# Three projection stages: transposes and matmuls by pairs of tiles, the bias on GpSimd, two banks for the heads' sums

## What is computed

```python
def _L0_attn_ref(x, qkv_w, qkv_b, proj_w, proj_b, rpb_table):
    ...
    attn = jax.nn.softmax(attn + bias[None], axis=-1)
    out = jnp.einsum('bhnm,bmhd->bnhd', attn, v).reshape(Bw, Nw, Cd)
    return out @ proj_w + proj_b
...
h = h + _L0_attn_ref(_layernorm(h, axis=-1), ...)      # stage prj
h = h + _L1_attn_ref(_layernorm(h, axis=-1), ...)      # linear attention, stage lpr
x = x + y @ wo.T                                       # causal attention in _L1_ffn_ref, stage cpj
```

## Time and profile before

| what | value |
|---|---|
| median of 3 runs | 2918.41 us (2917.83 to 2937.95) |
| profiled execution, own time | 2931.52 us |
| its span | 2929.7 us |
| TensorE busy (PE) | 2564.9 us, 88% |
| weight loads (PEld) | 1160.8 us, 40% |
| DVE, ScalarE (ACT), GpSimd (POOL) busy | 1987.7, 1552.4, 354.0 us |
| granted TensorE clock, mean | 0.887 of full speed |

### The profile page before, as it was taken

The page is one execution under the profiler, slowest core; times in us unless marked ns, Lnnn a source line. Parts: engine busy times, 40 slices in busy tenths (PEclk is TensorE's granted clock), DMA queues, the critical chain, the costliest instruction groups (busy, mean ns, idle before and its releaser), DMA issues. The chain is left out here.

```text
span 2929.7 us, 52672 instructions
## 1 busy us (share of the span) xinstructions
PE 2564.9 (88%) x18552; PEld 1160.8 (40%) x18552; DVE 1987.7 (68%) x5083; ACT 1552.4 (53%) x2645; POOL 354.0 (12%) x456
## 2 busy tenths in 40 slices
PE   5987659999999999997699997986679998789999
PEld 3323542333333333335333333564544444623333
DVE  5686668888888888871477775737667774256665
ACT  2332654777777777772244443615646666134443
POOL 1020100000000000003112211011101011221110
PEclk9998767999999999996699997755589999589999
DMA  2101991112212212213300001233422231511100
GB/s 72 22 15 27 279 281 51 48 45 55 56 38 56 55 38 55 70 17 85 67 17 17 22 16 24 61 85 124 160 104 72 66 91 35 123 28 29 29 15 20
DMA packets 308491, 188.23 MB, mean 64 GB/s; under 512 B 262069, under 2 KB 263414, under 8 KB 306982
## 3 DMA queue, kind: packets, MB, share of 16 engines
q1 hardware_dynamic: 297870, 165.80, 21.4%
q0 software_dynamic: 10368, 19.06, 2.1%
HBM read 103.16 MB, written 81.69 MB: 63 GB/s over the span
## 5 line engine op out<-in xcount | busy, mean ns | idle before, releaser
L1614 DVE TENSOR_REDUCE att_mpart<-ps 128x1 f32<-128x512 f32 x1024 | 637.3, 684 | 81.2 <-PE ps L1423 48.5
L1571 ACT ACTIVATE att_p<-ps 128x704 f32<-128x704 f32 x768 | 543.3, 760 | 139.5 <-PE ps L1487 134.5
L1516 PE MATMUL ps<-att_p,att_v 128*32 128x352 f32 x3072 | 308.4, 472 | 0.1
L1423 PE MATMUL ps<-att_kT,att_qT 64*128 64x512 bf16 x1024 | 274.5, 387 | 27.5 <-DMA att_qz<-qt_d 14.2
L1487 PE MATMUL ps<-att_qm,att_kT 64*128 64x352 bf16 x1536 | 251.1, 317 | 10.8 <-ACT att_p L1571 8.0
L1243 DVE TENSOR_REDUCE cau_mpart<-ps 128x1 f32<-128x512 f32 (+5 forms) x384 | 193.5, 552 | 90.8 <-PE ps L1069 70.7
L2285 ACT ACTIVATE mo_act<-ps,mo_b 128x768 f32<-128x768 f32 x176 | 156.3, 901 | 129.5 <-PE ps L2167 129.5
L2478 DVE TENSOR_TENSOR mo_g<-mo_act,ps 128x768 f32<-128x768 f32 x176 | 167.4, 951 | 79.5 <-PE ps L2202 43.5
L1210 ACT ACTIVATE cau_p<-ps 128x704 f32<-128x704 f32 (+6 forms) x272 | 171.6, 660 | 82.5 <-PE ps L1128 49.7
L2865 ACT ACTIVATE mo_act<-ps 128x1024 f32<-128x1024 f32 (+1 forms) x108 | 102.9, 953 | 196.3 <-PE ps L2779 196.0
L1487 PEld LDWEIGHTS ps<-att_qm,att_kT 64*128 64x128 bf16 x1536 | 82.4, 93 | 279.8 <-issue 263.6
(11 more groups left out here) (432 smaller groups left out, 4367.2 us busy)
## 6 DMA issues: line engine op xcount, KB each, us to landing
v_d<-pre_v SPq DMA_DIRECT2D x32, 288.0 KB, 4.3
qs_d<-pre_qs SPq DMA_DIRECT2D x8, 1152.0 KB, 5.6
att_qs<-qs_d SPq DMA_DIRECT2D x32, 288.0 KB, 4.5
att_v<-v_d SPq DMA_DIRECT2D x32, 288.0 KB, 4.4
qt_d<-pre_qT SPq DMA_DIRECT2D x8, 1056.0 KB, 4.4
kt_d<-pre_kT SPq DMA_DIRECT2D x8, 1056.0 KB, 7.6
att_kT<-kt_d SPq DMA_DIRECT2D x32, 264.0 KB, 2.7
att_qT<-qt_d SPq DMA_DIRECT2D x32, 264.0 KB, 3.1
```

The source lines that it names most:

```text
L1423: mm = pe.matmul(ps[:, bank, :], qT[half(s), u, j * P:(j + 1) * P], kT[half(s), u, c * BANK:(c + 1) * BANK], start=True, stop=not near)
L1516: mm = pe.matmul(ps[32 * cg:32 * cg + 32, 7, 0:TH], v[:, u, i, s, :], p[:, r, s, :], start=i < 2, stop=i == FULL - 1)
L1571: e = act.activation(p[:, n % PRING, :, :], ps[:, bank:bank + 2, 0:TH], ACT.Exp)
L1614: red = dve.tensor_reduce(mpart[:, j, s, c:c + 1], ps[:, bank, :], AX.X, ALU.max)
```

## The change

It changes `project` in five ways. (1) `turn` transposes two neighbouring tiles of `att` at once, 128 partitions by 128 columns: four transposes and a small one instead of eight and a small one. Of each pair, channels of the even tile land on partitions 0 to 63 and those of the odd one on 64 to 127, in one bank. (2) `back` weighs the two halves as two row tiles of the array: `w` is loaded to both halves of the partitions, the matmuls alternate between them, and their outputs go to banks 4 and 5. The number of matmuls stays. ScalarE copies 128 partitions by 512 and the small piece. (3) The ones and the bias row are gone; GpSimd adds the bias, spread over all partitions, into the residual rows before DVE needs them, and DVE waits for that. (4) The heads' sums get a second pair of banks, 6 and 7, by turns. (5) front(b + 1) stands ahead of turn(b).

```diff
...
@@ -1659,19 +1658,21 @@
         den = nm.sb("den", [P, 2, NT, heads])
         rden = nm.sb("rden", [P, 2, NT, heads])
         att = nm.sb("att", [P, 2, NT, C])
-        xT = nm.sb("xT", [P, 2, N])
+        xT = nm.sb("xT", [P, 2, BANK + TT])
         w = nm.sb("w", [P, C])
+        bias = nm.sb("bias", [P, C]) if bias_d is not None else None
...
         block = const["block"]
-        XT, Y = 2, 5
+        FRONT, XT, Y = (0, 6), 2, 4
+        PAIRS = FULL // 2
...
@@ -1697,9 +1698,10 @@
 
         def fetch(sp):
             load(sp, 0, 0)
-            sp.dma_start(w[0:C, :], w_in_d).then_inc(S["w_in"], 16)
+            for r in (0, C):
+                sp.dma_start(w[r:r + C, :], w_in_d).then_inc(S["w_in"], 16)
             if bias_d is not None:
-                sp.dma_start(w[C:KW, :], bias_d.rearrange("(o c) -> o c", o=1)).then_inc(S["w_in"], 16)
+                sp.dma_start(bias[:, :], bias_d.rearrange("(o c) -> o c", o=1).broadcast_to([P, C])).then_inc(S["w_in"], 16)
...
@@ -1736,23 +1738,34 @@
         @block.gpsimd
         def _(pool):
...
-            if bias_d is not None:
-                pool.memset(xT[C:KW, :, :], 1.0).then_inc(S["one_set"], 1)
-                pool.wait_ge(S["one_set"], 1)
 
             def add_parts(b, par):
 
                 arrived(pool, o_in, b, par, len(parts))
                 at_least(pool, S["ot_mm"], b - 1)
-                at_least(pool, S["sum_made"], b)
                 pool.tensor_tensor(osum[:, par, :], o[:, par, 0, :], o[:, par, 1, :], ALU.add).then_inc(S["sum_made"], 1)
+                pool.wait_ge(S["sum_made"], b + 1)
+
+            def add_bias(b, par):
+
+                arrived(pool, res_in, b, par, 2)
+                pool.tensor_tensor(res[:, par, 0:FULL, :], res[:, par, 0:FULL, :], bias[:, :].unsqueeze(1)
+                                   .broadcast_to([P, FULL, C]), ALU.add).then_inc(S["b_made"], 1)
+                pool.wait_ge(S["b_made"], b * 2 + 1)
+                pool.tensor_tensor(res[0:TT, par, FULL, :], res[0:TT, par, FULL, :], bias[0:TT, :], ALU.add)\
+                    .then_inc(S["b_made"], 1)
+                pool.wait_ge(S["b_made"], b * 2 + 2)
 
             if NO == 2:
                 add_parts(0, 0)
             tidy(pool, const)
-            if NO == 2:
-                for b in range(1, B):
-                    add_parts(b, b % 2)
+            if bias_d is not None:
+                pool.wait_ge(S["w_in"], 48)
+            for b in range(B):
+                if NO == 2 and b + 1 < B:
+                    add_parts(b + 1, (b + 1) % 2)
+                if bias_d is not None:
+                    add_bias(b, b % 2)
...
@@ -1765,44 +1778,43 @@
                     pe.wait_ge(S["sum_made"], b + 1)
                 else:
                     arrived(pe, o_in, b, par, len(parts))
-                at_least(pe, S["att_made"], b * 3)
+                at_least(pe, S["att_made"], (b - 1) * 3)
                 for t in range(NT):
                     src = osum[:, par, t * P:t * P + rows(t)] if NO == 2 else o[:, par, 0, t * P:t * P + rows(t)]
-                    mm = pe.transpose(ps[0:rows(t), t // 7, (t % 7) * HR:(t % 7 + 1) * HR], src,
+                    mm = pe.transpose(ps[0:rows(t), FRONT[par] + t // 7, (t % 7) * HR:(t % 7 + 1) * HR], src,
                                       const["eye"][0:HR, 0:HR])
                 mm.then_inc(S["ot_mm"], 1)
 
             def turn(b, par):
 
-                at_least(pe, S["xt_cp"], b * 3)
-                for t in range(NT):
-                    if t in (0, 7, 8):
-                        pe.wait_ge(S["att_made"], b * 3 + (0, 7, 8).index(t) + 1)
-                    mm = pe.transpose(ps[0:C, XT + t // 4, (t % 4) * P:(t % 4) * P + rows(t)], att[0:rows(t), par, t, :],
-                                      const["eye"][0:rows(t), 0:rows(t)])
-                    if t % 4 == 3 or t == NT - 1:
-                        mm.then_inc(S["xt_mm"], 1)
+                at_least(pe, S["xt_cp"], b * 2)
+                for m in range(PAIRS):
+                    if m in (0, PAIRS - 1):
+                        pe.wait_ge(S["att_made"], b * 3 + (1 if m == 0 else 2))
+                    mm = pe.transpose(ps[:, XT, m * P:(m + 1) * P], att[:, par, 2 * m:2 * m + 2, :].rearrange("p s c -> p (s c)"),
+                                      const["eye"][:, :])
+                mm.then_inc(S["xt_mm"], 1)
+                pe.wait_ge(S["att_made"], b * 3 + 3)
+                pe.transpose(ps[0:C, XT + 1, 0:TT], att[0:TT, par, FULL, :], const["eye"][0:TT, 0:TT]).then_inc(S["xt_mm"], 1)
 
             def back(b, par):
 
                 at_least(pe, S["hn_made"], b * 2)
-                for t in range(NT):
-                    if t % 4 == 0:
-                        pe.wait_ge(S["xt_cp"], b * 3 + t // 4 + 1)
-                    bank, col = Y + t // FULL, t % FULL * C
-                    mm = pe.matmul(ps[0:rows(t), bank, col:col + C], xT[0:KW, par, t * P:t * P + rows(t)], w[0:KW, :],
-                                   start=True, stop=True)
-                    if t >= FULL - 1:
-                        mm.then_inc(S["y_mm"], 1)
-
-            pe.wait_ge(S["w_in"], 16 * (1 if bias_d is None else 2))
-            if bias_d is not None:
-                pe.wait_ge(S["one_set"], 1)
+                pe.wait_ge(S["xt_cp"], b * 2 + 1)
+                for m in range(PAIRS):
+                    for s in range(2):
+                        mm = pe.matmul(ps[:, Y + s, m * C:(m + 1) * C], xT[s * C:(s + 1) * C, par, m * P:(m + 1) * P],
+                                       w[s * C:(s + 1) * C, :], start=True, stop=True)
+                pe.wait_ge(S["xt_cp"], b * 2 + 2)
+                pe.matmul(ps[0:TT, Y, PAIRS * C:(PAIRS + 1) * C], xT[0:C, par, BANK:BANK + TT], w[0:C, :], start=True, stop=True)\
+                    .then_inc(S["y_mm"], 1)
+
+            pe.wait_ge(S["w_in"], 16 * (2 if bias_d is None else 3))
             front(0, 0)
             for b in range(B):
-                turn(b, b % 2)
                 if b + 1 < B:
                     front(b + 1, (b + 1) % 2)
+                turn(b, b % 2)
                 if b > 0:
                     back(b - 1, (b - 1) % 2)
             back(B - 1, (B - 1) % 2)
@@ -1812,11 +1824,11 @@
...
             for b in range(B):
                 par = b % 2
-                at_least(act, S["y_mm"], (b - 1) * 2)
-                for c in range(3):
-                    n = min(4 * P, N - 4 * c * P)
-                    act.wait_ge(S["xt_mm"], b * 3 + c + 1)
-                    act.activation(xT[0:C, par, 4 * c * P:4 * c * P + n], ps[0:C, XT + c, 0:n], ACT.Identity).then_inc(S["xt_cp"], 1)
+                at_least(act, S["y_mm"], b - 1)
+                act.wait_ge(S["xt_mm"], b * 2 + 1)
+                act.activation(xT[:, par, 0:BANK], ps[:, XT, :], ACT.Identity).then_inc(S["xt_cp"], 1)
+                act.wait_ge(S["xt_mm"], b * 2 + 2)
+                act.activation(xT[0:C, par, BANK:BANK + TT], ps[0:C, XT + 1, 0:TT], ACT.Identity).then_inc(S["xt_cp"], 1)
 
         @block.vector
         def _(dve):
@@ -1824,8 +1836,8 @@
 
             def front(b, par):
                 dve.wait_ge(S["ot_mm"], b + 1)
-                at_least(dve, S["xt_mm"], (b - 1) * 3)
-                gots = [ps[0:rows(t0), t0 // 7, (t0 % 7) * HR:(t0 % 7 + t1 - t0) * HR].rearrange("p (a d) -> p a d", d=DV)
+                at_least(dve, S["xt_mm"], (b - 1) * 2)
+                gots = [ps[0:rows(t0), FRONT[par] + t0 // 7, (t0 % 7) * HR:(t0 % 7 + t1 - t0) * HR].rearrange("p (a d) -> p a d", d=DV)
                         for t0, t1 in SPAN]
...
@@ -1845,14 +1857,17 @@
                                       .broadcast_to([n, (t1 - t0) * heads, D]), ALU.mult).then_inc(S["att_made"], 1)
 
             def back(b, par):
-                arrived(dve, res_in, b, par, 2)
+                if bias_d is not None:
+                    dve.wait_ge(S["b_made"], b * 2 + 2)
+                else:
+                    arrived(dve, res_in, b, par, 2)
...
-                dve.wait_ge(S["y_mm"], b * 2 + 1)
-                dve.tensor_tensor(hn[:, par, 0:FULL, :], ps[:, Y, :].rearrange("p (t c) -> p t c", c=C), res[:, par, 0:FULL, :],
-                                  ALU.add).then_inc(S["hn_made"], 1)
-                dve.wait_ge(S["y_mm"], b * 2 + 2)
-                dve.tensor_tensor(hn[0:TT, par, FULL, :], ps[0:TT, Y + 1, 0:C], res[0:TT, par, FULL, :], ALU.add)\
+                dve.wait_ge(S["y_mm"], b + 1)
+                dve.tensor_tensor(hn[:, par, 0:FULL, :].rearrange("p (m s) c -> p s m c", s=2),
+                                  ps[:, Y:Y + 2, 0:PAIRS * C].rearrange("p s (m c) -> p s m c", c=C),
+                                  res[:, par, 0:FULL, :].rearrange("p (m s) c -> p s m c", s=2), ALU.add).then_inc(S["hn_made"], 1)
+                dve.tensor_tensor(hn[0:TT, par, FULL, :], ps[0:TT, Y, PAIRS * C:(PAIRS + 1) * C], res[0:TT, par, FULL, :], ALU.add)\
                     .then_inc(S["hn_made"], 1)
```

(8 more changed lines are left out.)

## The result

The changed kernel takes 2902.1 us in the median of 20 runs (2886.8 to 2914.9), the kernel before 2930.6 in as many (2914.7 to 2941.9). The ratio is 0.9906, 95% interval 0.9887 to 0.9926, some 27.6 us less. My forecast was 28.4 us less, within 1%, with 2890 us on the clock. That was counted down from the 2918.4 us of three runs of the kernel before; over 20 runs its median is 12 us higher, and that is why 2902 stands against 2890 although the difference is the forecast one.

The account below looks back on a forecast made before the run. A two-batch ring through SyncE's store and loads was taken to bound prj and cpj, TensorE to bound lpr. Gains of 7.6, 15 and 5.7 us sum to 28.3, giving 2890 us, rounded; range 2883 to 2898.

Parts of the forecast that it names:

- Part 1: In turn, four 128x128 transposes replace eight of 128x64: turn goes from 2.03 to 1.15 us.
- Part 2: In back, weight loads of the two row tiles run side by side, 16 loads in 8 steps: 1.76 us less.
- Rival B: In back, pairs do not run side by side, as only 64 columns stream: 2909.7 us; chance 0.13.
- Part 3: In back, 64 rows instead of 65: the height change costs 0.15 us; back goes from 3.71 to 2.1 us.
- Part 4: The new order puts turn into the chain from front(b+4) to hn(b+2): 4.4 us, against 4.9 before in prj.
- Part 5: Doubled sum banks: nothing in steady state; at a stage's start the DVE step between front(0) and front(1) goes.
- Part 6: Without the fill of ones, prj starts 1.9 us earlier and lpr 2.7 us (between 1.85 and 3.45).
- Part 7: GpSimd's bias adds, 1.7 us with waits, are hidden in prj; behind lpr, 7.05 us of zero fills lose their cover.
- Part 8: Extra weight load and broadcast bias are hidden in the prefetch; ScalarE's copies and DVE's large add unchanged within 0.1 us.
- Burst of transfers: In prj, two batches' transfers come 4.4 us apart: 1.4 us added to each second one (bounds 0 and 2.5).
- rival A: Bursts of transfers cost nothing, so prj and cpj gain 2.8 us each more: 2884.5 us; chance 0.20.
- rival C: Bursts collide: head loads land 2.5 us later in prj and cpj, 1.5 in lpr: 2897.5 us; chance 0.12.

Follow-up runs that it names:

- run 5: Changed kernel with all eight of back's matmuls per batch read from partitions 0 to 63, the odd tiles' outputs left out; ratio to the kernel before 0.9982.
- Run 12: Changed kernel with back's signal split again, so DVE's large add does not wait for the ninth tile; ratio to the kernel before 0.9888.
- Run 2: Changed kernel with turn(b) ahead of front(b + 1) again; ratio to the kernel before 0.9882.
- run 8: Changed kernel with turn(b) ahead of front(b + 1) and a single pair of banks for the heads' sums; ratio to the kernel before 0.9889.
- run 7: Changed kernel with the fill of ones put back into a spare tile, TensorE waiting for it; ratio to the kernel before 0.9885.
- run 4: Changed kernel, SyncE behind lpr waiting only for the zero fill of the tile it loads; ratio to the kernel before 0.9880.
- run 1: Changed kernel with back's two loops exchanged, all four even-tile matmuls before the four odd ones; ratio to the kernel before 0.9915.
- run 11: Changed kernel with next heads issued before stores, single fill wait, sums before bias, and old turn/front order in prj and cpj; 2858.6 us, ratio 0.9766.

## Why the prediction was right, point by point

- **Part 1, turn 1.15 us**: 1.18 (1363.23 to 1364.41). Right.
- **Part 2, pairs of weight loads, 1.76 us**: 16 loads took 3.48 us from one half, 1.78 from two: 1.70. Right, and it is nearly the whole change (run 5: 23.4 of 27.1 us). Rival B is the change without this overlap, which run 5 makes; I had put it at 8.7 us of gain, and it has 3.7. The Trainium skill ("TensorEngine Tiling (Array Packing)", Key Properties) has it that different tiles load and multiply in parallel and that a change of tile within a mode drains nothing; these 1.70 us agree.
- **Part 3, back 2.1 us**: wrong by 0.36. I subtracted from 3.71 us, a time in which the add did not wait for the ninth tile (the diff drops one of the two signals), and did not see that the new one does. Run 12 gives 0.32 of it back; its 2.14 us are 3.71 - 1.70 + 0.13, which leaves the 0.15 for the change of height standing, though no run has it alone. With the 0.36 us the even ring of prj took 16.6 instead of 16.1 us, and they are a part of why lpr's took 11.5 to 12.2 instead of 11.2.
- **Part 4, turn now lies in the ring**: right. Run 2 takes it out, and prj and cpj are 2.2 and 2.3 us shorter.
- **Part 5, the doubled bank**: nothing in the old order, as run 8 shows. In the new order, where front(b+1) stands ahead of the quotients of b, no run tests it alone.
- **Part 6, the fill**: right. 1.9 and 2.7 us forecast, 2.0 and 2.5 measured (run 7).
- **Part 7, bias and fills**: "That cover goes": it went, 7.42 us instead of 2.28 behind hn(7), 5.0 us of it go in run 4 and 1.57 when the last addition is left out (the two overlap and don't add up). Forecast for lpr was 15, measured 13.5: hn(0) to hn(5) took 28.3 us and not 27.2, hn(5) to the next load 14.2 and not 13.8. Run 12 gives back 1.0 of the 1.5.
- **Part 8, hidden work**: no run separates it; prj's start shortened by 3.0 us, as forecast (1355.6 to 1352.5).
- **Burst of transfers, 1.4 us on the second batch**: too much. hn(1) to front(5) took 12.38 us (1354.81 to 1367.19), hn(0) to front(4) 11.85, and in the next pair 12.55 against 11.81: 0.5 to 0.7 us. It made up for part 3, so that prj came out at 7.6 by two errors that cancel, which is luck: the odd ring was forecast 17.5 and took 17.15 and 17.31. The truth lies halfway between the 1.4 us and rival A, which put the burst at nothing; rival C's 2.5 us are excluded.
- **Rival D**: excluded, back is 2.46 and not 6.1.
- **A wrong number in its text**: the front at 1384.11 us, called front(4), is front(6), eight fronts having started at 1341.31, 1346.02, 1350.71, 1357.78, 1367.55, 1374.61, 1384.11 and 1391.34, and the heads loaded there are those of batch 6. The ring from hn(b) over front(b+4) to hn(b+2), with b = 2 in that row, and its 11.7 and 4.9 us are right.
- **The clock**: the prediction has 0.50 in all three stages. That held but for lpr's start, which had 1.00 in this profile and gave some 0.5 us that the change did not bring.

The mechanism was as forecast: 27.1 us in the stages for 28.3, with TensorE's overlap in lpr and the ring through the store in prj and cpj. The closeness to about 1 us is partly luck, by the errors that cancel in prj.

## What to carry to other kernels

Small fp32 matmuls that are paced by their weight loads went nearly twice as fast here when neighbours lay in different row halves of the array (16 loads in 1.78 us instead of 3.48). But the gain shows only where TensorE or the path through it is the bound: look first which queue closes the ring. A load that waits for a store only because both stand in one queue cost the changed kernel nearly as much as the whole change had gained (22.5 against 27.1 us) and the kernel before 10.5; with that wait gone, the same change was worth 39.1 us. Work moved to an idle engine is free only until something queued behind it, a sum or the next stage's fills, has to wait for the same transfer. When a change merges two signals, find out which consumer did not need the later one.

## What was not expected of the hardware

The two halves of the array work as two streams that need not be interleaved in the program: with eight weight loads for one half written ahead of eight for the other, the sixteen took 2.69 us (run 1), against 1.78 when written by turns and 3.48 in one half, so nearly half of the overlap came by itself. The Trainium skill ("TensorE: Matmul & The Clock Gate", Part 3, The mechanism) has weight loads pulled ahead where the rows differ, but matmuls in strict order. Back's group of matmuls, 2.88 us in run 1 against 3.67, is 0.8 shorter too, so whole pairs of load and matmul of the two halves ran beside each other. The records name no half, but their lengths mark where a half begins: in one half (run 5) only the first load and the first matmul of a group are of another length, 0.28 and 0.47 us instead of 0.33 and 0.42; written by turns, the first two are; and in run 1 the first and the sixth, in each of the 24 groups. So in run 1 the second half's first matmul started when three of the eight written ahead of it were still to come. By this reading of the lengths a matmul of one half does overtake those of the other, where the skill has none.

The linear attention between prj and lpr has the same code in all kernels, yet it took 93.5 to 118.0 us in 14 profiles, a spread of 24.5 us, where the 20 runs of the changed kernel spread over 28. Its stretch, from its first load to its last matmul, in the profiles of before, of after, and of runs 2 and 4 (columns as in run 11's rows above):

```profile
1802.50:1909.03 106.53, 92.57 (x456) 59.78 (x456) 71.13 (x344) 62.98 (x141) 3.77 (x7) 0.71 0.22 53
```

```profile
1793.26:1905.38 112.12, 99.63 (x456) 63.89 (x456) 71.25 (x344) 63.16 (x141) 3.75 (x7) 0.65 0.21 51
```

```profile
1789.70:1883.16 93.46, 75.09 (x455) 49.00 (x456) 70.75 (x344) 61.76 (x141) 3.75 (x7) 0.88 0.25 61
```

```profile
1791.12:1909.10 117.98, 106.95 (x455) 68.01 (x456) 71.47 (x344) 63.52 (x141) 3.75 (x7) 0.60 0.20 48
```

The same instructions take TensorE 75 to 107 us, at a mean granted clock of 0.88 to 0.60 of full speed: it is the share of the stage spent at 1.2 rather than 2.4 GHz that differs, and what decides it stays open. The profile of before has 106.5 us there, that of after 112.1, and that is the main reason why their spans differ by less (23.4 us) than the changed stages (27.1). In such a kernel single profiles are compared by stages, not by spans.
